# Natural scores every 0.040 of a half in place of 0.045, and the first half's key copies and differences every 0.060 in place of 0.045

## What is computed

```python
q = x @ Wq + 2.0 * (x @ Aq @ Bq)            # (16, 112, 1024)
k = ctx @ Wk + 2.0 * (ctx @ Ak @ Bk)        # (16, 375, 256), v alike
scores = einsum('bhqd,bhtd->bhqt', q, k) / sqrt(32)
attn = softmax(scores, axis=-1)
out = x + (context @ Wo + 2.0 * (context @ Ao @ Bo))   # context = attn @ v
```

## Time and profile before

| | |
|---|---|
| median of 3 runs | 1040.0 us (1038.49 to 1043.4) |
| the profiled execution's own time | 1043.98 us |
| its span | 1042.1 us |
| TensorE busy | 972.3 us, 93% |
| VectorE busy | 583.6 us, 56% |
| ScalarE busy | 433.5 us, 42% |
| GpSimd busy | 320.1 us, 31% |
| a step in the middle (two halves) | 38.5 us |

### The profile page before, as it was taken

How to read it: one execution, slowest core, us unless ns; L and a number is a source line. 1 busy time by engine, 2 the same in 40 slices (tenths; PEclk the granted TensorE clock), 3 DMA queues, 4 the chain that set the end, 5 groups by cost and what they waited for, 6 DMA issues and landing times.

```text
span 1042.1 us, 15943 instructions
## 1 busy us (share of the span) xinstructions
PE 972.3 (93%) x5904; PEld 802.1 (77%) x5904; DVE 583.6 (56%) x1005; ACT 433.5 (42%) x843; POOL 320.1 (31%) x276
## 2 busy tenths in 40 slices
PE   6989999977999999999999999999999767989998
PEld 4879999966887887887887877877878534768886
DVE  5661312257577676676677677667667643334321
ACT  3341211223555555555565565555655433201000
POOL 1201000000354354453453553553543545300000
PEclk9999999989899999999999999999999767989999
DMA  6739422643143443444344344245253442477652
GB/s 188 233 92 249 150 97 86 170 101 103 48 111 84 101 111 92 94 111 106 80 110 111 75 111 120 65 112 127 58 123 76 112 130 57 128 222 203 202 158 81
DMA packets 106004, 124.73 MB, mean 120 GB/s; under 512 B 30048, under 2 KB 89568, under 8 KB 105936
## 3 DMA queue, kind: packets, MB, share of 16 engines
q1 hardware_dynamic: 102076, 110.16, 41.3%
q10 hardware_dynamic: 3860, 13.67, 3.6%
HBM read 87.59 MB, written 29.82 MB: 113 GB/s over the span
## 4 chain that ended last, share of the span: by engine, by line
PE 74%; DVE 12%; DMA 5%; ACT 3%; issue 3%; SPq 1%; POOL 0%; ACTq 0%; DVEq 0%; POOLq 0%
PE ps L691 10%; PE ps L692 10%; PE ps L693 10%; PE ps L882 8%; PE ps L897 8%; PE ps L870 7%; PE ps L831 5%; PE ps L833 4%; PE ps L835 4%; PE ps L776 4%; DVE maxima L1268 4%; DVE k_stack L1197 3%; DMA q_scratch<-q_out_lo 3%; PE ps L932 2%; DMA out_dram<-residual 1%
## 5 line engine op out<-in xcount | busy, mean ns | idle before, releaser
L1268 DVE TENSOR_REDUCE maxima<-ps 112x1 f32<-112x375 f32 x512 | 269.2, 542 | 79.8 <-PE ps L882 71.2
L1060 ACT ACTIVATE probs<-ps 125x448 f32<-125x448 f32 x384 | 207.9, 543 | 170.1 <-PE ps L870 169.1
L671 POOL TENSOR_TENSOR prob_sum<-probs 125x448 f32<-125x448 f32 x128 | 146.0, 1156 | 343.4 <-ACT probs L1060 341.9
L882 PE MATMUL ps<-k_stack,q_stack 96*112 96x376 f32 x512 | 185.7, 363 | 21.9 <-DVE maxima L1268 20.3
L870 PE MATMUL ps<-q_stack,k_stack 97*125 97x448 f32 x384 | 146.8, 383 | 12.1 <-DVE a_stack_o L1146 4.3
L677 POOL TENSOR_TENSOR prob_sum<-prob_sum,probs 125x448 f32<-125x448 f32 x128 | 147.4, 1159 | 26.4 <-ACT probs L1060 24.9
L882 PEld LDWEIGHTS ps<-k_stack,q_stack 96*112 96x112 f32 x512 | 92.0, 180 | 46.1 <-DVE maxima L1268 42.0
L831 PE MATMUL ps<-wv_hi,ct_hi 128*125 128x256 f32 x384 | 112.6, 293 | 5.2 <-DVE k_stack L1197 5.2
L833 PE MATMUL ps<-wv_lo,ct_hi 128*125 128x256 f32 x384 | 109.4, 285 | 0.0
L835 PE MATMUL ps<-wv_hi,ct_lo 128*125 128x256 f32 x384 | 109.4, 285 | 0.0
L1191 DVE TENSOR_TENSOR ct_lo<-ps,ct_hi 128x375 fp32r<-128x375 f32 x128 | 70.2, 548 | 55.3 <-ACT ct_hi L997 55.3
(11 more groups left out here) (80 smaller groups left out, 1436.4 us busy)
## 6 DMA issues: line engine op xcount, KB each, us to landing
ctx_in<-in_ctx_dram SPq DMA_DIRECT2D x16, 1344.0 KB
q_stack<-q_scratch SPq DMA_DIRECT2D x96, 224.0 KB, 4.2
x_in<-in_x_dram SPq DMA_DIRECT2D x8, 896.0 KB, 8.7
q_scratch<-q_out_hi SPq DMA_DIRECT2D x16, 448.0 KB, 2.8
q_scratch<-q_out_lo SPq DMA_DIRECT2D x16, 448.0 KB, 3.7
attn_scratch<-attn SPq DMA_DIRECT2D x32, 224.0 KB, 4.1
attn_rows<-attn_scratch SPq DMA_DIRECT2D x14, 512.0 KB, 4.8
inv_tile<-inv_scratch SPq DMA_DIRECT2D x56, 128.0 KB, 5.1
```

What stands on the lines that cost most here:

```text
L882: mm = pe.matmul(ps[0:NQ, NAT + i % 2, 0:NTE], qst[nxt][0:STK, g, rr * NQ:(rr + 1) * NQ], kst[nxt][0:STK, g, :], start=True, stop=True)
L1060: act.activation(probs[:, c, j, :], ps[0:TR, score_bank(i), 0:QH], ACT.Exp, scale=SM).then_inc(exp_done, 1)
L1268: dve.tensor_reduce(maxima[:, h, i:i + 1], ps[0:NQ, NAT + i % 2, 0:NT], AX.X, ALU.max).then_inc(max_done, 1)
```

## The change

Two numbers of `PLAN` change, for both halves:

```diff
     + [("I", 0, 0.35), ("J", 0, 0.45)]
-    + [("N", i, 0.02 + 0.045 * i) for i in range(JH * RH)] + [("M", 0, 0.805)]
-    + [(f"{kind}0", j, 0.53 + 0.045 * j) for kind in "EF" for j in range(JH)]
+    + [("N", i, 0.02 + 0.04 * i) for i in range(JH * RH)] + [("M", 0, 0.805)]
+    + [(f"{kind}0", j, 0.53 + 0.06 * j) for kind in "EF" for j in range(JH)]
     + [(f"{kind}1", j, 0.82) for kind in "EF" for j in range(JH)],
```

## The result

The changed kernel takes **1059.6 us** (median of 6 runs, 1056.2 to 1062.5) against 1041.0 us (median of 6 runs of the kernel before beside it, 1038.5 to 1045.3): a ratio of 1.017, 95% interval 1.014 to 1.020, so 18.6 us slower. 1060 was forecast. Its profiled execution took 1057.7 us, its span is 1055.8 us.

What follows compares the result with a forecast made beforehand. TensorE, 90% or more busy in the middle, was taken as the bound, losing only by waiting. Thirteen steps at +1.62 us (21.1), plus 1.1, less 1.8 and 0.5, gave +19.9 on 1040.0: 1060 us, range 1049 to 1068.

Steps and rivals of the forecast that it cites:

- half 0, N11: Natural score 11 of half 0 waits for a maximum behind a transposed chunk's difference on VectorE: 0.25 us.
- half 0, N14: Natural score 14 of half 0 waits for a maximum right behind a transposed chunk's difference on VectorE: 0.78 us.
- half 1, N6: Natural score 6 of half 1 waits for a maximum behind a transposed chunk whose copy is delayed: 0.45 us.
- half 1, N11: Natural score 11 of half 1 waits for a maximum now behind the reciprocal on VectorE: 0.52 us.
- half 1, N15: Natural score 15 of half 1 waits for a maximum delayed by the first key difference: 0.80 us, as before.
- b = -1: Step without scores to attend; a third maximum ahead of the last key differences gains 1.8 us over both halves.
- b = 0: Step without a reciprocal, so without that wait of 0.52 us: 1.1 us slower.
- b = 14: Step whose half 1 has two maxima fewer behind the long wait for the first normalisation: 0.5 us gained.
- The faster one: Rival: waits at the end of half 1 go and closer scores find VectorE free; 1019 us, chance 0.06.
- The small loss: Rival: half 0's new waits overlap with what TensorE would lose at P anyway; about 1046 us, chance 0.08.
- No change: Rival: gains of half 1 and the first step cancel half 0's loss; 1040 us, chance 0.04.
- the clock rival: Rival: TensorE's clock falls to 1.2 GHz for a tenth of each step; 1087 us, chance 0.03.

Runs made afterwards that it cites:

- e7: Kernel before with the natural scores 0.04 apart in half 0 alone; 1051.8 us, ratio 1.011.
- e5: Changed kernel with the reciprocal moved from 0.35 to 0.66 of the half and its store from 0.45 to 0.76; 1053.3 us.
- e1: Changed kernel with key copies and differences back at their old spacing, so only the closer natural scores remain; 1061.0 us.
- e2: Changed kernel with natural scores back at their old places, so only the wider key copies and differences remain; 1037.0 us.
- e4: Changed kernel with natural scores due at 0.03 + 0.044 i and key copies and differences at 0.56 + 0.07 j; 1019.7 us.
- e10: The e4 kernel run once more with nothing changed; 1020.0 us, ratio 0.982.
- e8: The e4 kernel with the next context's load issued earlier, ahead of the key stack's transfer; 1016.0 us, ratio 0.980.

## Why the prediction was right

**Step by step.** The lost time of each wait, from the middle steps of the trace, against the forecast (with the 0.09 of a weight load that no matmul covers counted in):

| wait | forecast | measured |
|---|---|---|
| half 0, N11 | 0.25 | 0.24 |
| half 0, N14 | 0.78 | 0.71 |
| half 1, N3 | 0.28 | 0.27 |
| half 1, N6 | 0.45 | 0.38 |
| half 1, N11 | 0.52 | 0.46 |
| half 1, N15 | 0.80 | 0.80 |
| M | 0 | 0 |

All six long waits stand where they were forecast, in the order of their sizes; e7 shows half 0's share by itself, e5 N11's, e1 and e2 that the keys have no part in it. The step grew by 1.50, forecast 1.62. N14, N6 and N11 of half 1 were each 0.06 or 0.07 too high, 0.22 for the six together; that the step is only 0.12 off means that the short waits, which were to shrink by 0.12, hardly did, so two small errors cancel in part. For N14 and N6 the reason is seen at the T ahead: T1's difference started 1.15 after it (427.48 to 428.63), where 1.20 was worked out, and T6's 1.15 where 1.21 was, so ScalarE got free a little sooner than assumed. For N11 it is the maximum behind the reciprocal, which took 0.47 and not 0.545; the earlier trace rows had it, with two maxima in 0.92.

**The other steps.** b = -1 gave a gain of 1.5 at its second M (249.6 to 248.1; 1.8 forecast). b = 0 was forecast 1.1 slower and came out 0.7 quicker (27.5 to 26.8 in half 0, 19.5 to 19.6 in half 1). The clock accounts for that, not the order. Right behind the M of b = -1 the granted clock was 0.50 in the kernel before (250 to 252 us) and 1.00 in the changed one. In e2, whose half 0 has the scores of the kernel before, it was 1.00 there too (249 to 255 us), and this half took 25.6 us, 1.9 less than before; against e2 the changed kernel's is 1.2 slower, near the forecast. b = 14 gained 0.8 (0.5 forecast), but that isn't shown to be the maxima's: e1, whose list of TensorE in the half 1 of that step is the same, took 28.7 us for it, the changed kernel 28.0, the kernel before 28.8, at a mean granted clock of 0.65, 0.71 and 0.65. Altogether the last M starts at 859.7 in place of 843.2, +16.5, where 19.9 was forecast: 1.7 of the difference is the 13 steps, 1.8 is b = 0, and the other two cancel.

**The total.** That 1060 was met to half a microsecond is partly luck. The traces say +16.5 up to the last M; behind it the changed kernel's profiled execution took 196.1 us, that of before 198.9, in code that is the same, and so the two profiled executions differ by only 13.7. Part of that is the clock again: its mean was 0.970 over the 1042.1 us before and 0.974 over the 1055.8 us after, which makes 31.3 and 27.5 us of full clock lost, an estimate of 4 us in the changed kernel's favour. Executions of one kernel scatter by as much: the runs of before beside e5 to e7 lie between 1036.6 and 1046.9, the long ones at a mean granted clock of 0.969 to 0.970, the short ones at 0.976 to 0.977. The medians' +18.6 has +14.7 to +21.2 as its interval, and 16.5 lies in it.

**Weight loads.** By the Trainium skill (TensorE: Matmul & The Clock Gate, Architectural detail: the array is 16x 32x32, not 1x 128x128) a load could have been pulled ahead, and the result would be near 1055. The load of N14 starts at 429.69 with its matmul, 0.67 us idle, and N15's at 451.15 after 0.90:

```profile
429.69 0.17 PEld L882 LDWEIGHTS ps<-k_stack,q_stack 96*112 96x112 f32 x1 [0.67 <-DVE maxima L1268]
...
451.15 0.17 PEld L882 LDWEIGHTS ps<-k_stack,q_stack 96*112 96x112 f32 x1 [0.90 <-DVE maxima L1268]
```

It didn't come ahead; it is part of the wait. In kernel.py the wait (`at_least(pe, max_done, ...)`) stands ahead of the call that makes load and matmul, so here the load lies behind it in TensorE's list; what a load does whose matmul alone waits, no run here shows. The totals alone wouldn't have told the two apart: +16.5 in the traces lies between the +15 of that rule and the +19.9 of the sum.

**The rivals.** The faster one (1019) fell on its own point: the new waits came to over 1.3 a step, N14 and N11 first. Yet its number was reached in e4 by another order. The small loss (1046) needed the waits of half 0 to be hidden at P; they aren't, half 0 grew by the full 1.00, and P still waits for nothing but issue. No change needed N6 and N11 not to wait, and they do. In the steps that the clock rival was about, the clock didn't fall: 1.00 from 400 to 780 us in all three rows above, with waits of up to 0.9 us among them. The rule of the Trainium skill (TensorE: Matmul & The Clock Gate, A second HAM failure mode) that frequent short idling makes it swing isn't borne out by these steps. But the prediction's "70 of them, and no fall" is too strong: its 70 waits are counted from 254 us on, and the earlier trace rows has an 8 in the slice from 261 to 287 us. The last section shows that fall, and one behind short waits.

## What to carry to other kernels

When an order of work comes from due times, a spacing isn't a cost; what counts is which ready instruction ends up behind one that is still waiting on an in-order engine, and how soon somebody needs its buffer. So list the blocking instructions (here each transpose's difference, the reciprocal, the key differences), and for what stands right behind each compare its end with the time at which the matmul two buffers on is due: that took rows of a few microseconds of one trace and met each long wait here within 0.07 us, while VectorE's average of 55% said that there was room. Once such waits are gone, look at once for the next thing that is late (here a load that had always been in time), and try several phases of the same spacing before judging the spacing.

## What the runs showed of the hardware

In the middle steps one long wait did what many short ones didn't. The profiled execution of e10 has one half of 25.2 us (M at 514.7 and at 539.9). The context's transposes waited 3.5 us there and started at 528.5. Its waits for that load from 254 to 795 us, and three stretches around the place (us, then busy time and count of PE, PEld, DVE, ACT and POOL, granted clock, DMA share, GB/s):

```profile
PEld ps L776 <- DMA ctx_in<-in_ctx_dram: 6.3, 6, 3.5
```

```profile
514.00:528.00 14.00, 11.33 (x88) 8.27 (x87) 8.38 (x16) 6.88 (x14) 4.08 (x4) 0.99 0.85 195
528.00:535.00 7.00, 6.54 (x28) 6.33 (x29) 2.97 (x6) 2.21 (x5) 2.27 (x2) 0.53 0.08 22
535.00:540.00 5.00, 5.00 (x40) 4.72 (x38) 3.23 (x7) 3.44 (x8) 3.91 (x4) 1.00 0.00 0
```

From 514 to 528 us, the wait at its end, the DMA engines were 85% busy; then the granted clock was 0.53 over the next 7 us, about the lower of the two levels, 1.2 GHz, and it was back at 1.00 from 535 on. The many waits of up to 0.9 us in the changed kernel's steps from 400 to 780 us were followed by no fall, this one wait of 3.5 us was. The half lost 25.2 - 19.0 = 6.2 us, so the wait explains only 3.5 of it; the other 2.7 is of the size of what seven microseconds at 0.53 cost, 7 x 0.47 = 3.3. Why the load was late in that step alone wasn't settled.

It isn't one case. Early in the step b = 0 TensorE waits once for a stack that VectorE makes ready, 4.5 us in every run and 4.0 in e8 (the kernel before and the changed one alike):

```profile
PEld ps L870 <- DVE a_stack_o L1146: 4.5, 1, 4.5
```

In the kernel before this wait ends at 260.13. The granted clock is 0.50 from 260 to 265 us, where a weight load of L831 takes 0.33 us in place of 0.19, and 1.00 from 270 to 795. The other runs show the same fall at this place.

Short waits can't be called harmless either. At the end of the step b = -1 of the kernel before, TensorE waits 1.23 us for N15's buffer and then 1.18 at M, 2.3 us apart, and the clock is 0.50 from 250 to 252 us. e7 has the same two waits (1.23 and 1.17 us), and its clock stays at 1.00 from 249 to 255.5. So the same waits were followed by a fall in one execution and by none in the other; what decides isn't shown here.
